# A graph network's edge windows: turned features kept, index lists resident, paired transfers

## What is computed

```python
ea = edge_attr @ eencW + eencb                 # the same in every layer
def _genconv(x, src, dst, ea, W1, b1, lg, lb, W2, b2, t):
    m = jax.nn.relu(x[src] + ea) + EPS
    logits = m * t
    mx = jax.ops.segment_max(logits, dst, num_segments=N)
    e = jnp.exp(logits - mx[dst])
    denom = jax.ops.segment_sum(e, dst, num_segments=N)
    alpha = e / denom[dst]
    agg = jax.ops.segment_sum(m * alpha, dst, num_segments=N)
    h = (agg + x) @ W1 + b1
    return jax.nn.relu(_ln(h, lg, lb)) @ W2 + b2
```

## Time and profile before

| | us |
|---|---|
| runs shown: median of 3 (lowest, highest) | 12002.17 (11963.65, 12016.73) |
| the profiled execution's own time | 11994.87 |
| its span, first to last instruction | 11993.1 |
| set-up, to the first window's gathers | 144.0 |
| gathers of layer 1's windows, first to last | 2603.3 to 4882 |
| from the end of layer 3's windows to the end | 2232.1 |
| busy: PE, DVE, ACT, POOL | 5746.9, 5926.9, 3290.7, 6801.0 |

### The profile page before, as it was taken

How to read it: one execution, slowest core, us unless ns; L and a number is a source line. 1 busy time by engine, 2 the same in 40 slices (tenths; PEclk the granted TensorE clock), 3 DMA queues, 4 the chain that set the end, 5 groups by cost and what they waited for, 6 DMA issues and landing times. The chain is left out here.

```text
span 11993.1 us, 107333 instructions
## 1 busy us (share of the span) xinstructions
PE 5746.9 (48%) x30526; PEld 4148.6 (35%) x30526; DVE 5926.9 (49%) x7860; ACT 3290.7 (27%) x4928; POOL 6801.0 (57%) x6468
## 2 busy tenths in 40 slices
PE   2333434344433433433433434334433447888887
PEld 2333323233333322333333333233332334555554
DVE  4443434344444433443444434344443447888887
ACT  1332323233333322332333333223332332111110
POOL 5555555544555555455555554555555546888887
PEclk8666666666666666666666667666666668999998
DMA  4332323222223223222232322223222324555554
GB/s 121 95 88 80 93 82 93 80 66 86 88 87 96 86 81 88 71 84 82 88 88 88 93 86 75 74 86 94 87 88 82 90 84 97 96 92 98 94 94 84
DMA packets 849217, 1051.23 MB, mean 88 GB/s; under 512 B 559309, under 2 KB 598787, under 8 KB 847351
## 3 DMA queue, kind: packets, MB, share of 16 engines
q1 hardware_dynamic: 522594, 822.25, 20.8%
q0 software_dynamic: 322624, 224.55, 12.8%
q10 hardware_dynamic: 3916, 3.40, 0.1%
HBM read 612.22 MB, written 437.38 MB: 88 GB/s over the span
## 5 line engine op out<-in xcount | busy, mean ns | idle before, releaser
L675 POOL DMA_INDIRECT xg<-h_tab,idx x4992 | 4775.5, 957 | 4283.3 <-issue 2983.0
L709 PE MATMUL turn<-ident,ea 128*64 128x128 f32 x10368 | 1112.0, 398 | 3280.8 <-issue 1700.6
L907 DVE TENSOR_TENSOR_SCAN rx<-rp,carry,zl 128x1536 f32<-128x1536 bf16 (+1 forms) x224 | 740.7, 3307 | 3572.0 <-ACT zl L820 2843.5
L709 PEld LDWEIGHTS turn<-ident,ea 128*64 128x64 f32 x10368 | 975.1, 211 | 3417.0 <-issue 1744.8
L1201 POOL DMA_INDIRECT acc<-vm,tgt x1026 | 1597.0, 1557 | 381.8 <-issue 298.9
L828 ACT ACTIVATE st_all<-turn 128x512 f32<-128x512 f32 (+1 forms) x1344 | 751.3, 578 | 2316.5 <-remote 1789.0
L810 ACT ACTIVATE at<-turn 128x512 f32<-128x512 f32 (+1 forms) x672 | 374.8, 579 | 3178.8 <-remote 2430.6
L718 PEld LDWEIGHTS zl<-ident,xg 128*128 128x128 f32 x5184 | 849.2, 226 | 817.6 <-issue 740.2
L733 PE MATMUL turn<-ident,num 128*128 128x128 f32 x2592 | 630.5, 399 | 973.4 <-issue 737.5
L718 PE MATMUL zl<-ident,xg 128*128 128x128 f32 x5184 | 863.9, 310 | 381.1 <-issue 322.2
L715 PE MATMUL zl<-at,attrW 128*128 128x512 f32 (+1 forms) x1344 | 900.0, 755 | 230.1 <-issue 162.5
(11 more groups left out here) (254 smaller groups left out, 6962.4 us busy)
## 6 DMA issues: line engine op xcount, KB each, us to landing
sums<-st_all SPq DMA_DIRECT2D x416, 768.0 KB
ea<-in_edge_attr_dram SPq DMA_DIRECT2D x420, 384.0 KB
srcB<-src_flat SPq DMA_DIRECT2D x108, 768.0 KB
rp<-run_pen SPq DMA_DIRECT2D x420, 192.1 KB
xg<-h_tab,idx POOLq DMA_INDIRECT x4992
run_head<-zeros SPq DMA_DIRECT2D x216, 192.0 KB
hd<-run_head SPq DMA_DIRECT2D x108, 384.0 KB
run<-run_pen SPq DMA_DIRECT2D x108, 192.0 KB
```

The source lines that it names most:

```text
L675: g_.indirect_dma_start(xg[b][:, k, h, :], None, h_tab[:, :], bass.IndirectOffsetOnAxis(ap=idx[b][:, h, k:k + 1] if small is None else idx ...
L709: ins = pe.matmul(ps[6 + (b + gr) % 2][h * D:(h + 1) * D, j * P:(j + 1) * P], ea[b][:, h, gr * gt + j, :], ident[:, :], start=True, stop=True)
L907: link(v.tensor_tensor_scan(rx[:, 0:width], rp[b][:, 0:width], zl[:, 0:width], carry[:, 0:1], ALU.min, ALU.max))
```

## The change

- The turned features `at` get two buffers. In layer 0 SyncE stores them, as they are evicted, to a new table `feat`; in layers 1 to 3 the 24 transposes and three evictions are left out, and one load brings the turned features into the buffer of `ea` (seen as `turned`), from which TensorE takes them directly. For this the layer's code stands twice: layer 0, and a loop over 1 to 3.
- All full windows' index lists are loaded once into `idx_full` (places 52 and 53 hold those of windows 0 and 1 again). VectorE copies the 24 numbers per partition of window w + 2 into `idx[b]` just before the scan L907 of window w, and GpSimd waits for that copy.
- The penalties of a full window come by one broadcast transfer for both halves, the sums leave by one transfer.
- To make room, two arrays of the list preparation lie in the memory of `xin` and `x_acc`. So x is loaded only after the lists are stored, and `x_acc` and the rest of `xin` are cleared later, too.

```diff
+                    def keep_features(g, b, gt=GT):
+                        sp.wait_ge(at_sb, NG * (g + 1) + A0)
+                        sp.dma_start(feat_v[g, :, :, 0:gt * P], at[b][:, :, 0:gt * P]).then_inc(feat_out[b], 16)
+                    def load_penalties(g, w, b):
                         sp.wait_ge(max_ok, g + 1)
                         sp.wait_ge(l_ok, g + 1)
                         sp.sem_inc(load_go, 1)
-                        for h in range(2):
-                            sp.dma_start(rp[b][h * D:(h + 1) * D, :], run_pen[bass.ds(h * HALF + w * W, W + 1)]
-                                         .partition_broadcast(D)).then_inc(rp_in[b], 16)
+                        sp.dma_start(rp[b][:, :], pen_v[:, bass.ds(w * W, W + 1)].unsqueeze(1)
+                                     .broadcast_to([2, D, W + 1])).then_inc(rp_in[b], 16)
+                    def load(g, w, b, first):
+                        sp.wait_ge(z_ps, NG * g + NG - NG * 2 + Z0)
+                        if first:
+                            for h in range(2):
+                                piece = bass.ds(h * HALF + w * W, W)
+                                sp.dma_start(ea[b][:, h, :, :], edge_attr[piece, :].rearrange("(p k) f -> p k f", k=K)
+                                             ).then_inc(ea_in[b], 16)
+                        else:
+                            sp.dma_start(turned[b][:, :, :], feat_v[w]).then_inc(ea_in[b], 16)
+                        load_penalties(g, w, b)
...
+                    def load_lists(place, w0, w1):
+                        for h in range(2):
+                            begin = h * HALF + w0 * W
+                            sp.dma_start(idx_full[:, place:place + w1 - w0, h, :], src[begin:begin + (w1 - w0) * W]
+                                         .rearrange("(w p k) -> p w k", p=P, k=K)).then_inc(idx_full_in, 16)
...
                     def store(g, w, b):
                         sp.wait_ge(back_sb, BU * (g + 1) + BS0)
-                        for h in range(2):
-                            sp.dma_start(sums_v[h, w], st[b][:, h, :, :].rearrange("p k c -> p (k c)")
-                                         ).then_inc(st_out[b], 16)
+                        sp.dma_start(sums_v[w], st[b].rearrange("p h k c -> p h (k c)")).then_inc(st_out[b], 16)
...
-                    load(0, 0, 0)
-                    load(1, 1, 1)
-                    sp.wait_ge(pads_ok, 4)
+                    load_lists(0, 0, 2)
+                    load(0, 0, 0, True)
+                    load(1, 1, 1, True)
+                    sp.wait_ge(pads_ok, 3)
+                    load_lists(2, 2, FULLW)
+                    load_lists(FULLW, 0, 2)
                     load_small_lists()
...
+                    sp.wait_ge(out_lists, 16 * 5)
+                    sp.wait_ge(pads_ok, 4)
                     sp.dma_start(xin[0:N // NT, :, :].rearrange("p t d -> p (t d)"),
                                  x.rearrange("(p t) d -> p (t d)", t=NT)).then_inc(fx_in, 16)
...
                             for b in range(2):
-                                load(l * LW + 2 * i + 2 + b, 2 * i + 2 + b, b)
+                                load(l * LW + 2 * i + 2 + b, 2 * i + 2 + b, b, first)
+                                if first:
+                                    keep_features(2 * i + b, b)
                                 store(l * LW + 2 * i + b, 2 * i + b, b)
...
-                            g_.wait_ge(idx_in[b], 32 * (l * FULL_PAIRS + i + 1))
+                            g_.wait_ge(idx_ok, l * FULLW + w + 1)
...
-                        for gr in range(NG):
+                        first = isinstance(l, int)
+                        for gr in range(NG if first else 0):
...
-                            pe.wait_ge(at_sb, NG * g + gr + 1 + A0)
-                            pe.matmul(ps[gr][:, 0:gt * P], attrW[:, :], at[:, gr, 0:gt * P], start=True, stop=True)
+                            if first:
+                                pe.wait_ge(at_sb, NG * g + gr + 1 + A0)
+                            pe.matmul(ps[gr][:, 0:gt * P], attrW[:, :], (at if first else turned)[b][:, gr, 0:gt * P],
+                                      start=True, stop=True)
...
-                        for gr in range(NG):
+                        for gr in range(NG if isinstance(l, int) else 0):
...
+                            if gr == 0:
+                                a.wait_ge(feat_out[b], 16 * i + FT0)
...
+                    def next_lists(w, b):
+                        v.tensor_copy(idx[b].rearrange("p h k -> p (h k)"), lists[:, bass.ds(w * 2 * K, 2 * K)]).then_inc(idx_ok, 1)
...
                         v.wait_ge(l_ok, g + 1 + L0)
+                        if width == W:
+                            next_lists(w + 2, b)
...
+                    v.wait_ge(lists_ok, 1)
+                    v.memset(x_acc[:, :, :], 0.0)
+                    v.wait_ge(out_lists, 16 * 5)
+                    v.memset(xin[96:P, :, :], 0.0).then_inc(pads_ok, 1)
                     v.wait_ge(fx_in, 16)
...
+                    v.wait_ge(idx_full_in, 16 * 6)
```

More of the change, by code:

```diff
@@ L456, in gnn @@
             ea = [sb(f"ea{i}", [P, 2, K, D], F32, c) for i in range(2)]
-            at = sb("at", [P, NG, GC], F32, c)
+            at = [sb(f"at{i}", [P, NG, GC], F32, c) for i in range(2)]
+            turned = [e.rearrange("p h k d -> p (h k d)").rearrange("p (g c) -> p g c", c=GC) for e in ea]
             idx = [sb(f"idx{i}", [P, 2, K], I32, c) for i in range(2)]
+            idx_full = sb("idx_full", [P, FULLW + 2, 2, K], I32, c)
+            idx_ok, idx_full_in = sem("idx_ok"), sem("idx_full_in")
             idx_last = sb("idx_last", [P, LAST, 2, K // 2], I32, c)
@@ L510, in gnn @@
             xg_in = [[sem(f"xg_in{i}_{gr}") for gr in range(NG)] for i in range(2)]
-            ea_in, idx_in, rp_in, st_out = (
-                [sem(f"{n}{i}") for i in range(2)] for n in ("ea_in", "idx_in", "rp_in", "st_out"))
+            ea_in, rp_in, st_out = (
+                [sem(f"{n}{i}") for i in range(2)] for n in ("ea_in", "rp_in", "st_out"))
             z_ps, u_ok, l_ok, diff_ok, ex_ok, max_ok, sums_ok, back_ps, back_sb = (
@@ L526, in gnn @@
             BU = 2 * NG
-            idx_last_in = sem("idx_last_in")
+            idx_last_in, feat_out = sem("idx_last_in"), [sem(f"feat_out{i}") for i in range(2)]
+            FT0 = 16
             LAST_LISTS = sum(E - h * HALF - FULLW * W - s * W // 2 > 0 for s in range(LAST) for h in range(2))
@@ L653, in _ @@
                             store_nodes(k)
+                    layer(0, True)
+                    with sp.Fori(1, L) as l:
+                        layer(l, False)
                     sp.wait_ge(tab_out, 16 * MC * L + 16)
@@ L735, in back, with layer @@
                             ins.then_inc(back_ps, 1)
-                    with pe.Fori(0, L) as l:
+                    def layer(l):
                         g0 = l * LW
@@ L787, in _ @@
                                 ins.then_inc(o_ps, 1)
+                    layer(0)
+                    with pe.Fori(1, L) as l:
+                        layer(l)
                 @block.scalar
                 def _(a):
-                    a.wait_ge(pads_ok, 4)
+                    a.wait_ge(pads_ok, 3)
                     whole_rows = ROWS_REAL * W
@@ L798, in _ @@
                     a.sem_inc(u_ok, U0)
+                    for b in range(2):
+                        a.sem_inc(feat_out[b], FT0)
                     a.sem_inc(at_sb, A0)
@@ L836, in exponentials, with layer @@
                         a.activation(rx[:, 0:width], rx[:, 0:width], ACT.Exp, scale=-1.0).then_inc(ex_ok, 1)
-                    with a.Fori(0, L) as l:
+                    def layer(l):
                         g0 = l * LW
@@ L893, in _ @@
                                 a.activation(h_cur[:, cs, :], h_cur[:, cs, :], ACT.Relu).then_inc(h_ok, 1)
+                    layer(0)
+                    with a.Fori(1, L) as l:
+                        layer(l)
                 @block.vector
                 def _(v):
+                    lists = idx_full.rearrange("p w h k -> p (w h k)")
+                    v.wait_ge(idx_full_in, 32)
+                    for b in range(2):
+                        v.tensor_copy(idx[b].rearrange("p h k -> p (h k)"), lists[:, b * 2 * K:(b + 1) * 2 * K]).then_inc(idx_ok, 1)
                     v.sem_inc(max_ok, M0)
```

87 lines of the change are left out of this document (48 added, 39 removed).

## The result

The changed kernel takes 11366.33 us (median of 4 runs, 11338.29 to 11377.44) against 11982.91 (4 runs, 11963.56 to 12016.73) for the one before, run beside it: a ratio of 0.948, interval 0.945 to 0.951. The forecast was 11460, range 10300 to 12050. The profiled execution after has a span of 11336.5 us, 656.6 less than before.

The account below looks back on a forecast made before the run. Bound: a loop of waits closed by index lists queued on SyncE behind a store. Layers 1 to 3 -557, layer 0 +10, half windows -16, set-up +20, sum -543: 11452, plus 7 to the median, 11460 us; range 10300 to 12050.

Parts of the forecast that it names:

- 12.24 us gap: GpSimd's idle time before each layer 1 window's gathers, put down to index lists queued on SyncE behind a store.
- rival B: Full windows become gather-bound: pre-activation finishes inside the gathers, idle about 2.5 us, layer 0 gains too; about 10400 us, chance 0.23.
- idle 8.4: Layers 1 to 3: expected gap before each window's gathers in us, instead of 12.24; with the copy, -557 us.
- half windows: Windows at a layer's end, lists already resident: their wait shortens by 1.3 us each, -16 us in layers 1 to 3.
- one or two: Layers 1 to 3: of three pre-activation matmul groups, how many finish early, inside the gathers; part of choosing 8.4 us idle.
- the tail of the crawl and the cold clock: Layers 1 to 3's remaining gap: 4.2 us of TensorE slowness after gathers, and TensorE starting at half clock (11.7 us chain).
- I take 0 for the exchange and + 0.2: Layer 0: swapping the index wait for VectorE's copy costs nothing, the copy itself 0.2 us per window; +10 us.
- a later start of the gathers gives TensorE the fast time it lacks: Layer 0: reason why waiting for VectorE's later copy should not lengthen windows, supporting 0 for the exchange.
- Set-up: Before the first layer: later x load, about 9 us, and big list loads, 11 us; +20 us, bounds 5 and 50.
- Penalties (D): Rival: joined penalty transfer confined to two rings takes 8.7 us instead of 1.1; on the path 13010 us, chance 0.04.
- C: Rival: at window starts gathers no longer pause, runs join and TensorE stays slow longer; 12770 us, chance 0.10.
- E: Rival: the transposes back, which stay, close the loop, so windows still take 42.5 us; about 12020 us, chance 0.10.

Follow-up runs that it names:

- Lists alone: Changed kernel with features turned in every layer and none stored, so resident index lists and paired transfers only; 12293 us, ratio 1.024 to the kernel before.
- kernel of two penalty transfers: Changed kernel with each window's penalties again sent as two broadcast transfers instead of one; 11359 us, ratio 0.946 to the kernel before.
- features-only: Changed kernel with index lists loaded per window as before, keeping stored turned features and paired transfers; 11561 us, ratio 0.962 to the kernel before.
- spare transposes: Changed kernel with layers 1 to 3's 24 feature transposes put back, results unread and not evicted; 9168 us beside 9152, and 11893 beside 12015.

## Why the prediction was right, point by point

**The gap and its owner.** That the index list, queued on SyncE, closed the loop and that VectorE's copy would be late next is what the groups show. The condition under it wasn't seen: that the crawl itself, and with it the whole 12.24 us gap, belongs to a condition that a series meets or doesn't. Where it is absent, the kernel before is as rival B has it, bound by its gathers, without any change. The rows were taken in the crawling condition and the result's runs met the same one; that part was luck, since beside a kernel before of 9152 us the same forecast would have failed.

**Layers 1 to 3.** Forecast 38.84 us per window, idle 8.4; measured 37.94, 37.82 and 37.74, idle 7.5 to 7.7, inside the forecast's own range of 6.4 to 10.6. With the half windows it is -720 against the forecast's -573. The step "the first matmul of the pre-activation can follow the last transpose back inside the run" holds for all three groups, not the "one or two" that I priced: they are through by 3602.2. The idle time that is left, priced as "the tail of the crawl and the cold clock", is the tail in the form of signals that reach ScalarE some 4 us after the run, and behind it ScalarE's and VectorE's part of the chain, 4.2 us in the cycle shown; no matmul is left to be slowed by the clock. That the signals would be late though the matmuls are done I hadn't seen.

**Layer 0.** This is the term mis-sized: "I take 0 for the exchange and + 0.2". It is +1.13 us per window, +57.4 for the layer, against +10; the bounds, -200 to +320, held it. Lists alone show the same in all layers (43.8), so it is the exchange and not the store of the features. The argument that "a later start of the gathers gives TensorE the fast time it lacks" failed: a window with transposes has 204 instructions, and in layer 0 the single steps begin after some 117 of them however late the gathers start.

**The sum.** The windows of layers 1 to 3 gave 147 us more than forecast and layer 0 47 us less; with 16 us between and behind the layers, for which the sum has no term and whose cause wasn't looked for, the span fell by 656.6 against 543. So a part of two misses cancelled.

**Set-up.** Forecast +20, measured +22.1 at the first gather, by a different split. SyncE's issues in the set-up of the changed kernel, and last that of the lists in the kernel of two penalty transfers:

```profile
133.19 26.99 SPq L608 DMA_DIRECT2D idx_full<-in_src_dram  x4
160.21 3.20 SPq L617 DMA_DIRECT2D idx_last<-in_src_dram  x7
...
182.17 0.27 SPq L658 DMA_DIRECT2D xin<-in_x_dram  x1
...
134.14 14.95 SPq L608 DMA_DIRECT2D idx_full<-in_src_dram  x4
```

The lists' issue takes 27 us, not 11 (its bound was 33), and the gathers' first wait is for the small lists behind it. It isn't chance: it takes 26.6 to 28.3 us in all ten kernels that load these lists behind joined penalties, in both conditions, and 14.95 in the one that splits them. That kernel differs in nothing else, so some 12 us of the set-up are the price of the slow transfer issued just before, which the forecast had at 0. (The features-only kernel has no such lists; there it is the small lists' issue that takes 12.4 us instead of 3.2.) x goes out 23.0 us later than at 159.21 before, of which the wait for the lists' store is most, but lands in 12.5 us instead of 20.8; ScalarE's first eviction comes at 201.80, 15.2 later than the earlier trace rows.

**Penalties (D).** The transfer is slow, and hidden in the windows, though not in the set-up. By the trace's packet records the 128 rows of 3074 bytes take 8.7 us of a window (median) where they took 2.6 before (the prediction had 1.1), with 1.8 of them under way at a time in the mean instead of 8.7. The estimate for two rings was 8.7 us. So the trace agrees with the Trainium skill ("DMA: Bandwidth & Descriptors", Rules for kernel authors) that a small outermost dimension confines a transfer to at most as many engines. `keep` has no wait for it, and undoing it leaves the windows as they are.

**The rivals.** B (idle 2.5) didn't come: the late signals keep the gap. C didn't: the copy, late as it is, keeps the runs apart, and half of layer 1's windows take between 38.1 and 38.4 us. E is refuted by the changed kernel and the features-only one, whose transposes back stay and whose times fall. D's transfer came out slow and hidden, but for the 12 us of the set-up.

## What to carry to other kernels

When an engine's instructions come at one fixed slow pace in some stretches, ask first whether it always does that: an unchanged kernel run beside each series is what keeps two conditions apart, and a gain measured in one may not exist in the other. A buffer refilled by an engine in the middle of the chain puts the whole chain ahead of its reader, and two more buffers gave nearly as much again (ratio 0.942 to 0.948 down to 0.901) as the change had gained. A transfer that is slow and hidden in the loop can stand in the way elsewhere: the joined penalties lengthened the set-up's issues by 12 us. Take work out of the loop before moving a gate behind it: the same resident lists cost 1.3 us per window with the transposes in the loop and gained 2.2 without them.

## What the runs showed that was not expected

The crawl has two forms, both seen while gathers run 1.26 us apart and for some 4 us afterwards (median). TensorE's instructions come 0.70 us apart, or a multiple of it; in the kernels whose gathers wait for VectorE's copy and whose windows have transposes this begins after some 117 instructions. And TensorE's signals are recorded late: by 23 us in the rows of layer 0 above, by up to 51 us in the trace of the kernel before, where two windows join; there it starts after 71 instructions in the median. SyncE's issues take 0.70 us each in the same stretch, as in the earlier trace rows.

One explanation offers itself, that the engines run out of instructions and wait for more to be loaded. The trace speaks against a load by DMA: it records the packets that fetch instructions (queues of kind "instruction", 83 packets in the whole span of the kernel before), and from the 5th to the 50th window none starts in any layer of the kernel before, of the changed kernel, or of the spare transposes in either condition. The data packets don't slow down either: those of 6144 bytes took 234 ns (median) in the gap-free run of the spare transposes and 235 in the crawling one. So the cause of the crawl stays open. It is there or absent for a whole series, on the same chip too, and the kernel before takes 12000 us with it and 9150 without.
